# Aggregation's bias opens the PSUM banks; attention finds its cells first and weighs 21 selects sooner

## The reference, cut to what matters

```python
def _L0_gnn_ref(x, edge_index, W1, b1, W2, b2, Wl, bl):
    row, col = (edge_index[0], edge_index[1])
    xc = x[row]
    xn = x[col]
    h = jax.nn.relu(xc @ W1[:d] + xn @ W1[d:] + b1)
    mask = jax.nn.sigmoid(h @ W2 + b2)[:, 0]
    seg_sum = jax.ops.segment_sum(mask, row, num_segments=n)
    w = mask / (seg_sum[row] + 1e-09)
    agg = jax.ops.segment_sum(w[:, None] * xn, row, num_segments=n)
    deg = jax.ops.segment_sum(jnp.ones_like(mask), row, num_segments=n)
    out_emb = jnp.where((deg > 0)[:, None], 0.5 * x + 0.5 * agg, x)
    return jax.nn.relu(out_emb @ Wl + bl)
...
h = jnp.maximum(_layernorm(x, axis=-1), 0.0)
x = x + _L0_gnn_ref(h, edge_index, L0_gnn_W1, ...)
```

## Time and profile before

| | us |
|---|---|
| median of 3 runs | 5220.53 |
| runs | 5219.7 to 5224.7 |
| the profiled execution | 5217.05 |
| its span, first to last instruction | 5215.3 |

### The profile page before, as it was taken

The page is one execution under the profiler, slowest core; times in us unless marked ns, Lnnn a source line. Parts: engine busy times, 40 slices in busy tenths (PEclk is TensorE's granted clock), DMA queues, the critical chain, the costliest instruction groups (busy, mean ns, idle before and its releaser), DMA issues. The chain is left out here.

```text
span 5215.3 us, 49297 instructions
## 1 busy us (share of the span) xinstructions
PE 3667.5 (70%) x16004; PEld 1596.0 (31%) x16004; DVE 3813.6 (73%) x6354; ACT 844.8 (16%) x2430; POOL 3205.7 (61%) x3145
## 2 busy tenths in 40 slices
PE   1800246555555524999997799878988899879997
PEld 0400112212222211444443344333433344333443
DVE  4699477666666634666664888879887888879987
ACT  0100010000000005777773100010000100010000
POOL 5200326777777774344442677767777677767777
PEclk9999678878787767999997899989999999989998
DMA  9993364444444427999996544444444444444443
GB/s 370 408 417 127 82 171 150 140 136 132 131 137 130 130 61 143 214 218 219 215 217 137 159 142 133 133 127 137 136 129 129 137 135 130 136 131 138 143 134 100
DMA packets 364047, 846.90 MB, mean 162 GB/s; under 512 B 100487, under 2 KB 178029, under 8 KB 363613
## 3 DMA queue, kind: packets, MB, share of 16 engines
q0 software_dynamic: 140752, 316.84, 27.6%
q1 hardware_dynamic: 173646, 436.97, 23.5%
q10 hardware_dynamic: 49392, 89.94, 5.5%
HBM read 601.13 MB, written 242.36 MB: 162 GB/s over the span
## 5 line engine op out<-in xcount | busy, mean ns | idle before, releaser
L2365 PE MATMUL c_wide<-c_choice,c_parts 128*128 128x512 fp8e4 x8232 | 1879.8, 387 | 277.6 <-DVE c_odd L2450 136.6
L2239 POOL DMA_INDIRECT c_ring<-table,near x1288 | 1286.3, 999 | 448.0 <-issue 316.9
L2365 PEld LDWEIGHTS c_wide<-c_choice,c_parts 128*128 128x128 bf16 x8232 | 798.6, 99 | 1329.3 <-DVE c_odd L2450 195.8
L2450 DVE TENSOR_TENSOR c_even<-c_even,c_wide 128x1024 f32<-128x1024 f32 x672 | 815.3, 1213 | 7.2 <-DVE c_far L2528 1.3
L2450 DVE TENSOR_TENSOR c_odd<-c_odd,c_wide 128x1024 f32<-128x1024 f32 x644 | 781.4, 1213 | 53.4 <-PE c_wide L2365 50.8
L1514 PE MATMUL a_wide<-a_choice,a_parts 128*128 128x512 fp8e4 (+1 forms) x2058 | 492.3, 389 | 370.1 <-DVE a_hidden L1597 350.6
L1393 POOL DMA_INDIRECT a_ring<-table_a,near x430 | 463.3, 1077 | 288.5 <-issue 115.8
L1939 PE MATMUL b_agg<-b_mass,b_h_row 128*128 128x512 f32 (+1 forms) x1372 | 558.4, 557 | 100.7 <-DMA b_mass<-masks 100.6
L1889 ACT ACTIVATE b_mass<-b_onehot,mask_r 128x128 f32<-128x128 bf16 x2058 | 605.7, 388 | 123.7 <-DVE b_onehot L1960 79.7
L1859 POOL DMA_DIRECT2D b_mass<-masks x343 | 298.1, 920 | 448.2 <-ACT b_mass L1889 432.1
L1400 POOL DMA_INDIRECT masks<-a_value,a_cell x430 | 485.8, 1130 | 131.1 <-issue 130.8
(11 more groups left out here) (342 smaller groups left out, 2925.2 us busy)
## 6 DMA issues: line engine op xcount, KB each, us to landing
c_choice<-chosen SPq DMA_DIRECT2D x196, 896.0 KB
masks<-n_zeros SPq DMA_DIRECT2D x196, 784.0 KB, 7.9
b_mass<-masks POOLq DMA_DIRECT2D x343, 448.0 KB, 12.9
a_pick_row<-picks ACTq DMA_DIRECT2D x343, 256.0 KB, 3.8
chosen<-a_choice SPq DMA_DIRECT2D x49, 896.0 KB, 4.9
c_ring<-table,near POOLq DMA_INDIRECT x1288
c_source<-table SPq DMA_DIRECT2D x28, 448.0 KB, 5.5
a_ring<-table_a,near POOLq DMA_INDIRECT x430, 4.5
```

The lines of the kernel that those rows point to most:

```text
L2239: pool.indirect_dma_start(ring[:, at + j, :], None, table1[layer % 2], bass.IndirectOffsetOnAxis(of_u[:, j:j + 1], 0)).then_inc(landed[n % ...
L2365: last = pe.matmul(wide[q][:, lo_c:hi_c], parts[:, s, part, :], choice[e][:, s % CHUNK, lo_c:hi_c], start=(part == 0), stop=(part == 2))
L2450: dve.tensor_tensor(side[:, :], side[:, :], found, ALU.max).then_inc(taken, 1)
```

## The change

In attention A_LAG goes from 5 to -16, with no weighing before select 4 (A_FIRST): tile 0 is weighed after select 4, tile 1 after 14, tile 2 after 22, tile 48 after 327. POOL's gates on taken selects open 30 selects earlier (A_EARLY), and those that are not positive fall away. `find_cells` becomes VectorE's first work after one memset; it handles all tiles at once in lists padded to 25 places a tile (49 x 25 = 1225), with scratch that lies in the hidden buffers, which are made one tensor for it. SP issues the three small loads ahead of own rows 1 to 6. In aggregation the bias row is loaded seven times side by side, and each closing begins with two bias products of 512 and 384 columns that open both banks; the seven products with Wl add to them.

```diff
-        A_RING, A_FLOWS, A_LAG, A_BEHIND, A_PICKS = 38, 10, 5, 5, 6
+        A_RING, A_FLOWS, A_LAG, A_BEHIND, A_PICKS = 38, 10, -16, 5, 6
+        A_FIRST, A_EARLY = 4, 30
-        WEIGHED_AT = tuple(reduced_at(CAP, u, A_LAG) for u in range(TILES))
+        WEIGHED_AT = tuple(max(A_FIRST, reduced_at(CAP, u, A_LAG)) for u in range(TILES))
...
+        WIDEST = max(CAP)
+        PLACES_ALL = TILES * WIDEST
...
-                for a in range(1, RANGES):
-                    load_own(a)
                 sp.wait_ge(w2_clear, 1)
                 sp.dma_start(w2_col[:, WIDTH - 1:WIDTH], w2_in).then_inc(w_loaded, 16)
                 sp.dma_start(w2_row[:, :], bc(w2_in.rearrange("k o -> o k"), [P, D])).then_inc(w_loaded, 16)
                 sp.dma_start(b2[:, :], bc(b2_in.rearrange("(o n) -> o n", o=1), [P, 1])).then_inc(w_loaded, 16)
+                for a in range(1, RANGES):
+                    load_own(a)
...
-                        if g >= A_RING and g % 2 == 0:
-                            pool.wait_ge(taken, allowed_at(CAP, g, 0))
+                        if g >= A_RING and g % 2 == 0 and allowed_at(CAP, g, A_EARLY) > 0:
+                            pool.wait_ge(taken, allowed_at(CAP, g, A_EARLY))
...
+                    cells.did(dve.tensor_scalar(spare[:, :], iota_block[:, 0:WIDEST], float(ZERO_ROW + 1), None, ALU.add))
+                    cells.did(dve.tensor_copy(by_tile(to_node), near[:, :, 0:WIDEST]))
+                    cells.wait()
+                    cells.did(dve.memset(by_tile(inner)[:, :, WIDEST - 1:WIDEST], 0.0))
                     for u in range(TILES):
-                        mine = slice(FIRST[u], FIRST[u] + CAP[u])
-                        cells.did(dve.tensor_copy(to_node[:, mine], near[:, u, 0:CAP[u]]))
-                        cells.did(dve.tensor_scalar(spare[:, mine], iota_block[:, 0:CAP[u]], float(ZERO_ROW + 1), None,
-                                                    ALU.add))
+                        if CAP[u] < WIDEST:
+                            cells.did(dve.memset(by_tile(inner)[:, u, CAP[u] - 1:CAP[u]], 0.0))
...
+                    cells.did(dve.tensor_tensor_scan(run[:, :, :].rearrange("p u j -> p (u j)"), same[:, 0:PLACES_ALL],
+                                                     bc(ones[:, 0:1], [P, PLACES_ALL]), 0.0, ALU.mult, ALU.add))
...
-                    for u in range(TILES):
-                        mine = slice(FIRST[u], FIRST[u] + CAP[u])
-                        cells.did(dve.tensor_tensor(cell[:, mine], cell[:, mine],
-                                                    bc(row_at[:, u:u + 1], [P, CAP[u]]), ALU.bitwise_or))
+                    cells.did(dve.tensor_tensor(cell[:, :, :], cell[:, :, :], bc(row_at[:, :].unsqueeze(2), full),
+                                                ALU.bitwise_or))
...
                 dve.memset(w2_col[:, :], 0.0).then_inc(w2_clear, 1)
+                find_cells()
                 split(0, 0)
...
-                    if n == CHUNK:
-                        find_cells()
...
+                    for lo_c, hi_c in ((0, BANK), (BANK, RCOLS)):
+                        pe.matmul(agg[cb % 2][:, lo_c:hi_c], ones[0:1, :], bl_row[0:1, lo_c:hi_c], start=True, stop=False)
                     for c in range(RANGE):
-                        pe.matmul(product[cb % 2][:, c, :], emb_t[:, c * P:(c + 1) * P], wl[:, :], start=True,
-                                  stop=False)
-                        last = pe.matmul(product[cb % 2][:, c, :], ones[0:1, :], bl[0:1, :], start=False, stop=True)
+                        last = pe.matmul(product[cb % 2][:, c, :], emb_t[:, c * P:(c + 1) * P], wl[:, :], start=False,
+                                         stop=(c in (HEAD - 1, RANGE - 1)))
```

More of the change, by code:

```diff
@@ L1257, in gnn @@
             choice = [sb(f"a_choice{e}", [P, CHUNK, WCOLS], F8) for e in range(3)]
-            hidden = [sb(f"a_hidden{e}", [P, RCOLS]) for e in range(A_HIDDEN)]
+            hidden = sb("a_hidden", [P, A_HIDDEN, RCOLS])
+            over_hidden = hidden[:, :, :].rearrange("p e c -> p (e c)")
             mask_t = sb("a_mask_t", [P, RCOLS])
@@ L1261, in gnn @@
             value = sb("a_value", [P, CAP_ALL])
[L1262 to L1267, removed]
+            run = sb("a_run", [P, TILES, WIDEST])
+            cell = sb("a_cell", [P, TILES, WIDEST], I32)
+            spare = sb("a_spare", [P, WIDEST])
+            same = over_hidden[:, 0:PLACES_ALL + 1]
+            inner = over_hidden[:, PLACES_ALL + 1:2 * PLACES_ALL + 1]
+            to_node = over_hidden[:, 2 * PLACES_ALL + 1:3 * PLACES_ALL + 1]
             row_at = sb("a_row_at", [P, TILES], I32)
@@ L1608, in copy_masks, with by_tile @@
                                       TINY, None, ALU.max).then_inc(masks_copied, 1)
+                def by_tile(ap):
+                    return ap.rearrange("p (u j) -> p u j", j=WIDEST)
                 def find_cells():
-                    cells.did(dve.memset(inner[:, :], 1.0))
-                    cells.did(dve.memset(same[:, :], 0.0))
+                    full = [P, TILES, WIDEST]
+                    cells.did(dve.memset(inner, 1.0))
+                    cells.did(dve.memset(same[:, 0:1], 0.0))
@@ L1628, in find_cells @@
+                    cells.did(dve.tensor_scalar(inner, same[:, 1:PLACES_ALL + 1], -1.0, 1.0, ALU.mult, ALU.add))
                     cells.wait()
-                    cells.did(dve.tensor_tensor(same[:, 1:CAP_ALL + 1], same[:, 1:CAP_ALL + 1], inner[:, :], ALU.mult))
+                    cells.did(dve.scalar_tensor_tensor(to_node, to_node, fast[:, :], inner, ALU.mult, ALU.mult))
                     cells.wait()
-                    cells.did(dve.tensor_tensor_scan(run[:, :], same[:, 0:CAP_ALL], bc(ones[:, 0:1], [P, CAP_ALL]),
-                                                     0.0, ALU.mult, ALU.add))
@@ L1633, in find_cells @@
-                    cells.did(dve.tensor_scalar(inner[:, :], same[:, 1:CAP_ALL + 1], -1.0, 1.0, ALU.mult, ALU.add))
-                    cells.did(dve.tensor_tensor(to_node[:, :], to_node[:, :], spare[:, :], ALU.subtract))
+                    cells.did(dve.tensor_tensor(cell[:, :, :], by_tile(to_node), bc(spare[:, :].unsqueeze(1), full), ALU.add))
                     cells.wait()
-                    cells.did(dve.scalar_tensor_tensor(to_node[:, :], to_node[:, :], fast[:, :], inner[:, :], ALU.mult,
-                                                       ALU.mult))
@@ L1638, in find_cells @@
-                    cells.wait()
-                    cells.did(dve.tensor_tensor(cell[:, :], to_node[:, :], spare[:, :], ALU.add))
-                    cells.wait()
-                    for u in range(TILES):
-                        mine = slice(FIRST[u], FIRST[u] + CAP[u])
-                        cells.did(dve.tensor_tensor(cell[:, mine], cell[:, mine],
-                                                    bc(row_at[:, u:u + 1], [P, CAP[u]]), ALU.bitwise_or))
+                    cells.did(dve.tensor_tensor(cell[:, :, :], cell[:, :, :], bc(row_at[:, :].unsqueeze(2), full),
+                                                ALU.bitwise_or))
```

29 lines of the change are left out of this document (18 added, 11 removed).

## The result

| us | before | after |
|---|---|---|
| median of runs | 5220.11 | 5158.38 |
| runs | 5215.96 to 5224.7 | 5155.18 to 5158.92 |
| the profiled execution (its span) | 5217.05 (5215.3) | 5155.18 (5153.4) |

The ratio is 0.988, with a 95% interval of 0.9863 to 0.9897: the changed kernel is 61.7 us faster. The forecast was 88 us; the time lies inside the range given.

A forecast was written before the change was run, and what follows sets the result against it. POOL's indirect DMAs were taken to bound attention, the PE aggregation, with DMA engines full. Attention -77 and closing -12 made -89 us on 5217.05, 5128; with the median 3.5 us above, 5132 us, range 5108 to 5182.

The forecast's parts named there:

- Part 1, the stalls: Attention: weighing and gates earlier remove POOL's 90.0 us of stalls, leaving 5 us, 0 to 35.
- The mark of 768 us for the first store: Attention, sign to check: POOL's first store should come near 768 us instead of 858.
- Part 1, POOL's own pace: Attention: POOL's DMAs slow beside VectorE work that formerly ran in POOL's idle time; 5 us lost, 0 to 25.
- the 12 us first taken for 30 selects: Attention: some 30 selects moved beside busy POOL cost it 0.40 us each, 12 us, before 5 was taken.
- the rule that was weighed there: Attention: two-port tensor_scalar and POOL instructions exclude each other wholly; 30 compares could cost 23 us in place of 5.
- Part 1, the end: End of attention: far_slots ready about 1 us after POOL's end, delaying the far gathers; 3 us lost, 0 to 15.
- Part 2: Start of attention: find_cells first in padded lists takes 17 us, SP's order brings first select near 691; by themselves 0.
- By themselves 0: Start of attention: find_cells first and SP's order only change when VectorE is ready, already counted with the earlier weighing.
- Part 3: Aggregation's closing: 2 us saved in each of six, 1.7 in the last; -12 us taken, between 0 and -23.
- rival (c): Aggregation: the closing gives nothing because the DMA engines are full; 5144 us, chance 0.12.
- (b): Attention, tiles 2 to 9: POOL still waits for selects held by early weighings, half the stall stays; 5172 us, chance 0.15.
- (d): Attention: POOL slows where it no longer idles, deciding from 1.51 us a DMA; kernel slower, 5252 us, chance 0.07.

The follow-up runs named there:

- the schedule alone: Kernel before with only A_LAG -16, A_FIRST 4 and A_EARLY 30; find_cells and SP's order stay old: 5155.69 us, ratio 0.9889.
- The run with the sum: Changed kernel whose select compare, still a tensor_scalar, also writes its row's sum to a scratch: 5072.98 us, ratio 0.9737 to the kernel before.
- hardly any compare: Changed kernel with VectorE's compare cut to 8 of its 1024 columns from select 21 on: 5069.09 us in one execution.
- the run with two inputs: Changed kernel whose compare is a tensor_tensor with the 128 numbers as a repeated second operand: 5305.53 us, ratio 1.0184 to the kernel before.
- short transfers: Kernel before with mass-block transfers cut from 896 to 512 columns: 5200.76 us with the old closing, 5165.48 us with the new.

## Why the prediction came out as it did

The forecast was 5132 us, 26 us too low: attention by 7, aggregation by 9, and 10.6 us are the stage of maxima, which the change doesn't touch.

**Part 1, the stalls: right.** The 90.0 us were POOL's, and 5.7 us are left where 5 were forecast. Both parts of the reason show in the runs: the schedule alone gives 57 us, and the last stall, ahead of the last pair of tile 5's gathers, is the one named (select 23). The mark of 768 us for the first store was missed by 12 us.

**Part 1, POOL's own pace: the term that was mis-sized.** 5 us were taken, 0 to 25. In four profiles of the old attention the last store ends at 1966.0 us in the mean, in three of the new at 1893.0: 73 us gained where 85 us of stall went, so 12 us were lost to slower DMAs. Some 9 of these lie in the first 37 gathers (they end at 726.0 instead of 716.7): seven gathers beside find_cells take 10.9 us where 6.6 would be undisturbed, and two beside tile 0's weighing, whose two 3.49 us steps have two inputs, take 3.80 and 3.22 us instead of 0.94 each. Before, both pieces of work stood almost wholly in POOL's long wait (716.7 to 780.5 us) and cost it nothing. The step that failed is the one that counted only the selects as work that comes out of POOL's idle time; it put find_cells and tile 0's weighing at nothing. It then set 12 us down to 5 because 860 x 1.408 is today's total, but that total holds this work where it is free. That the 12 us first taken for 30 selects is also what was measured is luck. The 0.40 us a select was good as an average, but in the window 1000 to 1800 it is made of 0.27 us for the compare (59 us in 219 selects) and 0.14 for the weighing.

On the rule that was weighed there: the compare costs POOL 0.27 to 0.29 of its 0.77 us on average, not the whole. Yet the rows at 1029 to 1043 us bear out that the two exclude each other: a compare that comes first holds the DMA to its own end, and one that begins while a DMA holds the memory is held itself, for some 0.1 to 0.2 us. The mean is lower because the two overlap only in part: a held DMA loses 0.30 us (59 us in 199), as the two shown lose 0.45 and 0.42. The Trainium skill ("SBUF — State Buffer", Who interferes with whom) excepts the form of tensor_scalar that writes its accumulator. The run with the sum agrees: 1.00 us a DMA, as with hardly any compare. The same section of the Trainium skill lets two inputs from SBUF contend with POOL's reads; the run with two inputs agrees, with 0.77 of 1.21 us.

**Part 1, the end: wrong, in size only.** 3 us were set aside for far_slots; SP was in time and nothing was lost.

**Part 2: right in its estimates, too brief in its sum.** find_cells takes 16.0 us (17 forecast) and ends at 683.9 (686), and the first select is taken at 691.75 (691). "By themselves 0" holds only where part 1 has counted them: alone they are worth 17 us, because select 25 comes sooner, and the full change ends some 8 us ahead of the schedule alone (1893 against 1901.38). Moving find_cells out of a stretch in which it was free for POOL also cost POOL the 4.3 us named above.

**Part 3: rival (c) is what happened.** -12 us were taken; the loop gave 0 (+2.3 here) and the last closing 3.6 us (VectorE waits 6.72 instead of 10.29; 1.7 forecast). The two gains in it were both set too low: per closing the PE saves 5.6 us rather than 2 when blocks are in time, and 3.6 instead of 1.7 in the last one (the closing shown takes 4.9 us, where 6.5 to 8 were forecast). Seven products in a row take 3.35 us, 0.48 each, even at half clock in the last closing, where the sum kept 0.72 for each as in the alternating order. And the block behind a closing no longer runs at half clock. And all of the gain inside the loop goes into the wait for mass blocks (24.5 us). The reason against (c) was "no wait of the PE for a mass block". That showed that the PE was the later of two nearly equal limits, not how far off the other was. The row that tells it was in the trace: the first range, without any closing, took 117.1 us, longer than those with one, and the PE waits for blocks there. The window of the earlier trace rows began behind it.

**Rivals (b) and (d): out.** One stall of 5.98 us stayed, not 40. POOL's DMA takes 1.42 us in mid-stage (800 / 565), under the 1.51 us from which (d) decides. The run with two inputs shows what (d) would have looked like: at 1.60 us (800 / 499) the stage is 157 us longer and the kernel slower than before.

## What to carry to other kernels

- Before a gain is booked on an engine that never waits, look at the stage's other full resource in a stretch where that engine has less to do; here the first range had no closing and told the price of the transfers.
- An engine that is slowed by another one's instructions is best priced by instruction form, from the single rows in which the two meet. An average per step (0.40 us) mixed compares with weighing steps, and hid that a slower form (1.27 us instead of 0.77) costs the other engine nothing and makes the stage some 75 us shorter.
- Stages that a change doesn't touch vary too (13 us in 2326 here): look at several profiles before their difference is put down to the change.

## What the runs showed of the hardware

- VectorE's compare in 0.77 us costs POOL's DMA issues 0.29 us in the mean; with the row's sum (1.27 us) nothing that shows; with a second input from memory (1.21 us) 0.77 us. The compare and the DMA issue exclude each other: a held issue ends about 0.8 or 0.12 us after the compare (199 of 565 in the window 1000 to 1800), and 27 of the 219 compares there, begun while an issue held them, take 0.85 to 0.97 us instead of 0.75. The faster instruction was the dearer one for the kernel: the sum form makes it 5073 us, the compare on ScalarE in two passes 5060 us, both faster than either kernel of this study.
- With the new closing the granted clock of the PE is higher: 0.98 in the window 2080 to 2745 instead of the 0.94 of the earlier trace rows, and so it is with short transfers, where no wait for blocks is in the way (0.98 against 0.94). The block behind the second range's closing takes 1.72 instead of 3.35 us. Why the clock falls less isn't settled by these runs.
